# Masks, one-hot and class table in bfloat16, the table in three parts, and the class product in the middle of a split

## The reference, cut to what matters

```python
h = jnp.maximum(_layernorm(x, axis=-1), 0.0)          # x: 32 x 256 x 1024
x = x + _L0_gnn_ref(h, adj, b1, adj, b2)              # adj: 256 x 256, used as W1 and W2

def _construct_adj(x, k):                             # x: 8 x 256 x 1024 in the names
    fv = x.mean(axis=1)
    nf = fv / jnp.linalg.norm(fv, axis=1, keepdims=True)
    sim = nf[:, :, None] * nf[:, None, :]
    _, idx = jax.lax.top_k(sim, kk + 1)
    idx = idx[..., 1:]
    adj = jnp.zeros((Bn, Nn, Nn), x.dtype).at[b_ix, r_ix, idx].set(1.0)
    adj = jnp.maximum(adj, jnp.swapaxes(adj, 1, 2))
    adj = adj.at[:, d, d].set(1.0)
    return adj

def _gc(x, adj, W, b):
    deg = adj.sum(axis=2, keepdims=True)
    deg = jnp.where(deg == 0, jnp.ones_like(deg), deg)
    h = x @ W.T + b
    return jnp.einsum('bij,bjh->bih', adj / deg, h)

adj = _construct_adj(x, K)                            # K = 8
h = jax.nn.relu(_gc(xr, adj, W1, b1))                 # xr: the last two axes swapped
h = _gc(h, adj, W2, b2)
```

## Time and profile before

| | |
|---|---|
| median of 3 runs | 516.86 us (516.5 to 517.17) |
| the profiled execution's own time | 516.86 us |
| its span in the profile | 515.0 us |
| TensorE, matmuls | 485.7 us busy, 94% |
| TensorE, weight loads | 334.0 us, 65% |
| VectorE | 367.8 us, 71% |
| GpSimd | 371.9 us, 72% |
| ScalarE | 339.1 us, 66% |
| chain that ended last | PE 86%, DVE 7%, ACT 2%, DMA 2%, POOL 1% |

### The profile page before, as it was taken

The page is one execution under the profiler, slowest core; times in us unless marked ns, Lnnn a source line. Parts: engine busy times, 40 slices in busy tenths (PEclk is TensorE's granted clock), DMA queues, the critical chain, the costliest instruction groups (busy, mean ns, idle before and its releaser), DMA issues.

```text
span 515.0 us, 7290 instructions
## 1 busy us (share of the span) xinstructions
PE 485.7 (94%) x2416; PEld 334.0 (65%) x2416; DVE 367.8 (71%) x858; ACT 339.1 (66%) x692; POOL 371.9 (72%) x342
## 2 busy tenths in 40 slices
PE   1974999899999999999999999999999999999996
PEld 0253667667776677767777677767777677776774
DVE  4899797989776977779776978769776764522334
ACT  3844988547778577766778676775778655555551
POOL 0182658666888877787888777787887788778773
PEclk9995899899999999999999999999999999999999
DMA  8892274355656365565565465664624243444424
GB/s 315 305 405 91 81 292 183 146 208 227 257 200 232 152 252 202 233 227 197 194 238 214 192 252 205 246 247 162 251 93 164 86 178 150 164 164 164 163 83 163
DMA packets 27701, 102.74 MB, mean 199 GB/s; under 512 B 2064, under 2 KB 2576, under 8 KB 27664
## 3 DMA queue, kind: packets, MB, share of 16 engines
q1 hardware_dynamic: 27280, 101.23, 51.6%
q0 software_dynamic: 384, 1.05, 0.5%
HBM read 68.72 MB, written 33.55 MB: 199 GB/s over the span
## 4 chain that ended last, share of the span: by engine, by line
PE 86%; DVE 7%; ACT 2%; DMA 2%; POOL 1%; issue 1%; SPq 0%; DVEq 0%; POOLq 0%; ACTq 0%
PE ps L589 46%; PE ps L595 23%; PE ps L619 5%; PE aux L556 5%; PE aux L651 3%; DVE stats L715 2%; DMA xin<-x 2%; PE aux L578 1%; DVE code_r L779 1%; PE ps L626 1%; ACT r L355 1%; PE aux L565 1%; DVE onehot L788 1%; ACT hb L321 0%; POOL h_lo L449 0%
## 5 line engine op out<-in xcount | busy, mean ns | idle before, releaser
L460 POOL TENSOR_TENSOR r_lo<-r,r_hi 128x512 fp32r<-128x512 f32 x128 | 167.7, 1332 | 88.6 <-ACT r_hi L378 84.2
L449 POOL TENSOR_TENSOR h_lo<-hb,h_hi 128x512 fp32r<-128x512 f32 x128 | 166.8, 1326 | 7.9 <-ACT h_hi L341 7.8
L892 DVE SCALAR_TENSOR_TENSOR res<-ps,bias,res 128x512 f32<-128x512 f32 x128 | 90.1, 746 | 66.5 <-PE ps L626 66.4
L321 ACT ACTIVATE hb<-xin,nmean,rstd 128x1024 f32<-128x1024 f32 x64 | 79.0, 1235 | 52.7 <-DVE nmean L736 52.7
L589 PE MATMUL ps<-r_hi,w_hi 128*128 128x512 f32 x256 | 109.7, 429 | 1.9 <-ACT r_hi L370 1.9
L589 PE MATMUL ps<-r_hi,w_lo 128*128 128x512 f32 x256 | 102.6, 401 | 0.0
L589 PE MATMUL ps<-h_hi,w_hi 128*128 128x512 f32 x256 | 101.9, 398 | 0.0
L589 PE MATMUL ps<-h_hi,w_lo 128*128 128x512 f32 x256 | 101.2, 395 | 0.0
L361 ACT ACTIVATE r<-ps,beta 128x512 f32<-128x512 f32 x64 | 43.5, 684 | 63.5 <-PE ps L619 63.5
L715 DVE BATCH_NORM_STATS2 stats<-xin 128x6 f32<-128x512 f32 x128 | 78.9, 676 | 5.4 <-DMA xin<-x 5.4
L595 PE MATMUL ps<-h_lo,w_hi 128*128 128x512 f32 x256 | 73.4, 408 | 0.0
(11 more groups left out here) (87 smaller groups left out, 543.8 us busy)
## 6 DMA issues: line engine op xcount, KB each, us to landing
res<-x SPq DMA_DIRECT2D x32, 1024.0 KB, 4.8
xin<-x SPq DMA_DIRECT2D x31, 1024.0 KB, 7.3
out<-res SPq DMA_DIRECT2D x31, 1024.0 KB, 4.0
xin<-x SPq DMA_DIRECT2D x2, 512.0 KB, 3.8
out<-res SPq DMA_DIRECT2D x4, 256.0 KB, 2.1
w<-w_t SPq DMA_DIRECT2D x1, 256.0 KB, 8.2
cst<-small SPq DMA_DIRECT2D x1, 229.5 KB, 5.5
xg<-x_t,rows POOLq DMA_INDIRECT x8, 5.7
```

The costliest lines, as they stand in the source:

```text
L321: last = nc.scalar.activation(hb[:, a, kf], xin[:, b % NX, kf], ACT.Relu, bias=nmean[:, kf, e:e + 1], scale=rstd[:, kf, e:e + 1], accum_ou ...
L449: last = nc.gpsimd.tensor_tensor(h_lo[:, kf, n], hb[:, b % NH, kf, n], h_hi[:, kf, n].bitcast(F32), ALU.subtract)
L460: last = nc.gpsimd.tensor_tensor(r_lo[:, kf, n], r[:, kf, n], r_hi[:, kf, n].bitcast(F32), ALU.subtract)
L892: nc.vector.scalar_tensor_tensor(res[:, b % NR, m, n], bank[m][:], bias2[:, m:m + 1], res[:, b % NR, m, n], ALU.add, ALU.add).then_inc(out ...
```

## The change

- `onehot`, `mask`, `tab` and `v_hi` are bfloat16 instead of fp32r.
- As bfloat16 holds 8 bits of a value, the table comes in three parts on 24 rows of each quadrant instead of two on 16: `cls`, `less` and `rows_of` are widened, a constant `less2` is new, `src3` holds three copies, the class matmuls have 24 weight columns instead of 16. `table` has four instructions instead of two, each waiting for the one before: `v_hi` from V2, the difference to `REST` in PSUM, `v_mid` from `REST`, and `tab`.
- `products(t+1)` on GpSimd stands between the two instructions of `split_h(t+2, 0)`, from pass 2 to the pass before the last but one, rather than after them; `tables` goes to the front of its pass.
- `group_twin` and `group_counts` also write a sum (`beside`), which nothing reads.
- The last element of `code_r` takes one of its operands from `ZERO` in PSUM, written by an additional instruction in `top_first`, instead of from `code` in SBUF.

```diff
--- before.py
+++ after.py
-        ("cls", np.where(row < 16, row % 8, -1.0)[:, None]),
-        ("less", np.where((row >= 8) & (row < 16), -1.0, 0.0)[:, None]),
+        ("cls", np.where(row < 24, row % 8, -1.0)[:, None]),
+        ("less", np.where((row >= 8) & (row < 24), -1.0, 0.0)[:, None]),
+        ("less2", np.where((row >= 16) & (row < 24), -1.0, 0.0)[:, None]),
...
-        onehot = sb("onehot", [P, 2, 2, N], F32R)
+        onehot = sb("onehot", [P, 2, 2, N], BF16)
...
-        mask = sb("mask", [P, P], F32R)
+        mask = sb("mask", [P, P], BF16)
...
+        beside = sb("beside", [P, 2])
...
-        src3 = sb("src3", [P, KF, 2 * NCLS])
-        v_hi = sb("v_hi", [P, P], F32R)
-        tab = sb("tab", [P, P], F32R)
+        src3 = sb("src3", [P, KF, 3 * NCLS])
+        v_hi = sb("v_hi", [P, P], BF16)
+        v_mid = sb("v_mid", [P, P], BF16)
+        tab = sb("tab", [P, P], BF16)
...
+        REST = aux[:, 2 * P:3 * P]
+        ZERO = aux[:, P + K_TOP:P + K_TOP + 1]
...
         def rows_of(b, m):
             a = 32 * ((b % G + 2 * m) % G)
-            return slice(a, a + 2 * NCLS)
+            return slice(a, a + 3 * NCLS)
...
-            def split_h(b, h):
+            def split_h(b, h, between=None):
                 n = half_of(h)
                 pool.wait_ge(hhi_ready, nth(b, h))
                 for kf in range(KF):
+                    if kf == 1 and between is not None:
+                        products(between)
...
             for t in range(-1, LAST):
+                if t > 0 and (t + 1) % G == 0:
+                    tables((t + 1) // G)
                 if t == 1:
                     gather(1)
                 split_r(t + 1, 0)
-                if t == 1:
-                    products(2)
-                if t >= 0 and t + 2 < NB:
-                    split_h(t + 2, 0)
-                if t > 0 and (t + 1) % G == 0:
-                    tables((t + 1) // G)
-                if t != 1:
+                if 1 < t < LAST - 1:
+                    split_h(t + 2, 0, t + 1)
+                else:
+                    if t == 0:
+                        split_h(2, 0)
                     products(t + 1)
+                    if t == 1:
+                        split_h(3, 0)
                 split_r(t + 1, 1)
...
-                nc.vector.tensor_scalar(STAT, fv[:, 1:K_TOP + 1], 0.0, 6.0, ALU.is_equal, ALU.add).then_inc(static_ready, 1)
+                nc.vector.tensor_scalar(STAT, fv[:, 1:K_TOP + 1], 0.0, 6.0, ALU.is_equal, ALU.add)
+                nc.vector.tensor_scalar(ZERO, fv[:, 0:1], 0.0, 4.0, ALU.is_equal, ALU.add).then_inc(static_ready, 1)
...
-                nc.vector.scalar_tensor_tensor(code_r[:, N - 1:N], fv[:, 0:1], 0.0, code[:, 0:1], ALU.min,
+                nc.vector.scalar_tensor_tensor(code_r[:, N - 1:N], fv[:, 0:1], 0.0, ZERO, ALU.min,
...
-                nc.vector.tensor_scalar(cnt_d[:], c_("pick_n"), cnt[:], None, ALU.mult).then_inc(cntd_ready, 1)
+                nc.vector.tensor_scalar(cnt_d[:], c_("pick_n"), cnt[:], None, ALU.mult, ALU.add,
+                                        accum_out=beside[:, 0:1]).then_inc(cntd_ready, 1)
...
-                last = nc.vector.tensor_scalar(onehot[o, k % 2, 1], code_r[q], c_("cls")[q], None, ALU.is_equal)
+                last = nc.vector.tensor_scalar(onehot[o, k % 2, 1], code_r[q], c_("cls")[q], None, ALU.is_equal, ALU.add,
+                                               accum_out=beside[o, 1:2])
...
-                    src3[:].rearrange("p k (d c) -> p k d c", d=2),
-                    prod[:].unsqueeze(2).broadcast_to([P, KF, 2, NCLS, NSRC]), AX_X, ALU.add).then_inc(src3_ready, 1)
+                    src3[:].rearrange("p k (d c) -> p k d c", d=3),
+                    prod[:].unsqueeze(2).broadcast_to([P, KF, 3, NCLS, NSRC]), AX_X, ALU.add).then_inc(src3_ready, 1)
...
                 nc.vector.tensor_copy(v_hi[:], V2).then_inc(vhi_ready, 1)
-                dve.wait_ge(vhi_ready, b + 1)
-                nc.vector.scalar_tensor_tensor(tab[:], v_hi[:].bitcast(F32), c_("less"), V2,
-                                               ALU.mult, ALU.add).then_inc(tab_ready, 1)
+                dve.wait_ge(vhi_ready, 3 * b + 1)
+                nc.vector.scalar_tensor_tensor(REST, v_hi[:], c_("less"), V2, ALU.mult, ALU.add).then_inc(vhi_ready, 1)
+                dve.wait_ge(vhi_ready, 3 * b + 2)
+                nc.vector.tensor_copy(v_mid[:], REST).then_inc(vhi_ready, 1)
+                dve.wait_ge(vhi_ready, 3 * b + 3)
+                nc.vector.scalar_tensor_tensor(tab[:], v_mid[:], c_("less2"), REST, ALU.mult, ALU.add).then_inc(tab_ready, 1)
```

More of the change, by code:

```diff
@@ L444, in _, with products @@
         def _(pool):
-            def split_h(b, h):
+            def products(b):
+                e, gp, g = b % RB, (b // G) % 2, b % G
+                shape = [P, KF, NCLS, NSRC]
+                pool.wait_ge(mix_ready, b // G + 1)
+                pool.wait_ge(r_ready, 2 * nth(b, 1))
+                if b > 0:
+                    pool.wait_ge(src3_ready, b)
+                nc.gpsimd.tensor_tensor(
+                    prod[:], src2[:, :, e].unsqueeze(2).broadcast_to(shape),
+                    mix[:, gp, g].unsqueeze(1).broadcast_to(shape), ALU.mult).then_inc(prod_ready, 1)
+            def split_h(b, h, between=None):
                 n = half_of(h)
```

## The result

The changed kernel took 521.79 us (median of 4 runs, 520.39 to 523.36) against 517.01 for the kernel before beside it (516.5 to 517.22): a ratio of 1.0097 (its 95% interval [1.0071, 1.0124]), 4.8 us slower. The profiled execution of it is the one of 520.39, 1.4 under the median, with a span of 518.6; before it was 515.0 in 516.86.

What follows compares the result with a forecast made beforehand. TensorE was taken to bound the kernel from about 105 us on. Terms 11.7 - 1.7 + 0.2 + 0.8 - 2.3 = +8.7 us, on a span of 515.0 plus 1.9 around it, gave 525.6 us; range 519 to 531.

Steps and rivals of the forecast that it cites:

- Table chain: Two added dependent VectorE instructions ahead of tab, 0.65 us for both against 0.31 of slack: +11.7 us over all batches.
- Ordinary steps: Table chain in 13 batches such as 2, 3, 7, 11: 0.34 us of new waiting each, 12 counted, 4.1 us.
- batches 4, 8, ...: Table chain where VectorE comes late out of the search: 0.87 us in each of five batches, 4.35 us.
- batches 5, 9, ...: Table chain where the earlier product frees v_hi: terms at 2.03 instead of 2.08, five times -0.05, -0.25 us.
- Quads: The 62 groups of four added-term matmuls, now bfloat16: 0.03 us less each, less 0.2 where VectorE sets the time, -1.7 us.
- Rival 1: In the quads, bfloat16 weights load about twice as fast, gaining 0.08 us a quad rather than 0.03: 522.5 us; chance 0.20.
- Rival 3: In the 62 quads, bfloat16 loses most of the 0.39 that is not stream, 0.25 each: 512.0 us, faster; chance 0.10.
- V2: Class matmuls load 24 columns instead of 16, hidden but for the first of each step: +0.2 us (0 to 0.6).
- Start: First two twins take longer with a sum beside them, so masks and all behind come later: +0.8 us (0.3 to 3).
- Group 1: Shorter code_r element and cnt_d nearly close TensorE's 2.15 us wait and avoid the half clock: net -2.3 us (0 to -4).
- Rival 2: Group 1's gain fails: another wait takes the place of cnt_d and the clock falls anyway: 527.9 us; chance 0.15.
- Moves on GpSimd: tables ahead of a split that waits anyway, products in mid-split with cover for the work queued behind: 0 us.

Runs made afterwards that it cites:

- e1: The kernel before with one-hot, mask, v_hi and tab in bfloat16 only, still two parts on 16 rows (third part missing from the result): 509.79 us, ratio 0.988.
- e3: The kernel before with only ZERO in PSUM and the sums beside cnt_d and the twins: 514.88 us, ratio 0.9977.
- e4: The changed kernel with GpSimd's loop of the kernel before (tables and products where they stood): 523.93 us, ratio 1.0145.
- e5: The changed kernel without the sums beside cnt_d and the twins, ZERO kept: 522.18 us, ratio 1.0109.
- e6: The changed kernel with code in SBUF back in place of ZERO, the sums kept: 521.84 us, ratio 1.0096.
- e2: The kernel before with the four-instruction table chain in fp32r on 16 rows, table still made from v_hi: 528.24 us, ratio 1.0225.
- e8: The kernel before with class matmuls in mid high product, and VectorE's reduction ahead of the search, its end a pass later: 515.47 us, ratio 0.9984.
- e7: The changed kernel with class matmuls in mid high product, and VectorE's reduction ahead of the search, its end a pass later: 509.61 us, ratio 0.9863.
- e9: The changed kernel with only VectorE's reordering: reduction ahead of the search, end of the search after table: 518.88 us, ratio 1.0034.
- e10: The changed kernel with only TensorE's reordering: class matmuls in the middle of the high product: 514.95 us, ratio 0.9963.

## Why the prediction was right, and where it was off

I forecast 525.6 us (519 to 531), slower with 0.85. It is slower, within the range, and 3.8 us less than forecast. The direction came by the mechanism forecast, a longer chain in front of the terms. That the number is no further off is in part luck: the quads gained 5.0 us more than forecast, and the chain cost 1.8 more. By steps:

- **Table chain: +11.7 forecast, +13.5 measured** (the shifts of the terms over batches 0 to 30, summed, without batch 2). The mechanism held in every kind of step. The two instructions added 0.72, not 0.65: the subtraction takes 0.36 and the cast 0.29, and each gap is 0.04. Ordinary steps lost 0.43 (I said 0.34), batches 0 and 1 0.73 (0.65), batches 4, 8, ... 0.82 (0.87), batch 24 0.56 (0.56), batches 5, 9, ... 0.03 (-0.05), batches 6, 10, ... 0.40 (0.33), batch 31 nothing. Groups of instructions by form in the changed kernel, columns as in the earlier trace rows:

```profile
L887 DVE TENSOR_REDUCE src<-prod 128x48 f32<-128x432 f32 x32 | 19.2, 599 | 9.5 <-POOL prod L458 9.5
...
L895 DVE SCALAR_TENSOR_TENSOR aux<-v_hi,cst,aux 128x128 f32<-128x128 bf16 x32 | 11.4, 356 | 1.1
...
L636 PEld LDWEIGHTS ps<-onehot,tab 24*128 24x128 bf16 x128 | 6.0, 90 | 16.2 <-DVE tab L899 15.5 <-issue 0.7
```

The third copy in the reduction cost the 0.15 that I gave it (599 against 450 ns). The waits of TensorE on VectorE in the changed kernel (us, times, longest):

```profile
PE ps L636 <- DVE tab L899: 5.2, 8, 1.5
...
PE aux L661 <- DVE src L887: 0.6, 1, 0.6
```

I had said that it would show some 25 waits of 0.35. This view alone would have misled: it shows 5.2 us in 8 waits, since the pipelined masks still count as busy while the terms wait. The weight loads' idle time before the terms, 15.5 us, is nearer to it, and the distances between starts tell it.
- **Quads: -1.7 forecast, -6.7 measured.** This is the step that failed. The sum took 0.03 a quad "near the lower end, because the drains and the fp32r load behind the quad stay". They do stay: the matmul behind the quad, whose 0.50 against 0.40 I had priced, still takes 0.50 in e1. What went is the same wait in the quad's own matmuls, 0.49 in the earlier trace rows: they take 498 ns on average before and 385 in e1, and terms to next product is 0.32, not the 0.39 to 0.42 that I said the profile would show. The quad's own load falls from 183 to 90 ns, which covers most of that; no run separates the rest, about 0.02, from faster streaming. Rival 1 named the mechanism and still halved the wrong thing: some 0.10 of the load of 0.18 stood bare, so a load shorter by 0.09 takes away nearly the whole wait on the way into the quad and none on the way out, where the load is still fp32r. Its 522.5 is near the 521.79 measured, but other terms had a share in that. The rule of the Trainium skill cited there ("TensorE: Matmul & The Clock Gate", Weight-path perf modes) speaks of about 2x, and the trace agrees, 183 to 90 ns. Rival 3 (0.25 a quad, the other side) did not come: 0.108 is short of its 0.17.
- **V2: +0.2**, measured 31 x 0.007 = 0.2; it is contained in the shifts of the terms above.
- **Start: +0.8 forecast, none in the profile.** The first masks came 12.41 after the codes instead of 11.53, as said, but the class matmuls of batch 0 stood at 55.76 against 56.15: a stretch of half clock of the same length, 17.1 us, had begun and ended 1.4 earlier. Counted from the codes they came at 20.16, before at 20.29. In e3 and e4, which have the same sums, the stretch ended at 55.82 and 56.64, as late as before (55.88) or later, and the 0.8 was paid: 21.04 and 21.13.
- **Group 1: -2.3 forecast, -2.3 measured** (batch 2 to batch 3, 18.55 to 16.25), with what I named next in line: VectorE's reduction now comes last (102.33) and the class matmuls wait 0.6 for it. The exact agreement is luck. By e5 and e6 ZERO and the sum on `cnt_d` are 1.8 of it; the absence of the half clock is some 0.7 (I said 1.4), by e1; the late table of batch 2 takes 0.4 back, and two quads give 0.2. That the edits kept the clock up isn't shown. TensorE had idled 2.15 us for `cnt_d` in the kernel before, 1.73 in e2 and 2.18 in e8, and the clock fell behind it; in e1 it idled 2.26 and the clock did not fall. Rival 2 fell, as the clock stayed at full in 96.20 to 100.00 and the wait that came in the place was 0.6 us.
- **Moves on GpSimd: 0 forecast outside batches 5, 6, ..., which held.** I credited it with curing the lateness of batches 5 and 6 and their like. e2 and e4 show that the longer steps cure most of that by themselves: in e4 all of it in batches 6, 10, ... and half in 5, 9, ... (`v_hi` at 1.01 instead of 1.38). Its gain at batch 28 (0.7 us) I hadn't seen.

By stretches the two profiles differ by -0.39 us up to the class matmuls of batch 0, +1.13 from there to those of batch 2, -2.30 to batch 3, +5.34 to batch 31 and -0.22 to the end: +3.56, where I forecast +8.7. The longest stretch closes by its terms: 12.05 for the chain in batches 3 to 30, less 6.05 for 56 quads, less 0.64 for the wait at batch 28, is 5.36. So the change trades 6.4 us of cheaper weight loads for some 12 of a longer chain, and stays slower because the chain ended just ahead of its consumer: 0.31 of slack for 0.72 of new work.

## What to carry to other kernels

Price an added dependent instruction at its consumer: its duration less the slack there, in each kind of step, and then look again at which other waits the longer step has healed, since two latenesses in one loop don't add up. Where a type change needs more preparation, move the producer earlier in the same edit (e7): that turned 4.8 us of loss into 7.2 of gain. For an operand type that the trace doesn't have, subtract what the load would lose from the part of it that stands bare, rather than scale the wait, and look at the matmuls that use this load, not at the ones behind them.

## What was unexpected of the hardware

- A weight load of 128 columns in bfloat16 takes 90 ns, in fp32r 183 to 190. Between the terms and the next product that is worth 0.108 us, though the product behind loads fp32r as before.
- While GpSimd works, a VectorE instruction on a single element with both tensors in SBUF took 1.17 to 1.18 us; with one of them in PSUM it took 0.14. With GpSimd idle (126.29 us in the kernel before) both in SBUF took 0.15. `cnt_d`, 32 elements, took 0.92 to 1.11 plain in group 1 and 0.24 to 0.25 with a sum written beside it.
- That sum has a price elsewhere: 1024 elements took 1.27 us with it, and at the start two plain ones took 0.98 together in bfloat16 (1.51 in fp32r); a plain one takes 1.45 where GpSimd works.
- The start holds a stretch of half clock in every profile (37.4 to 54.5 us in the changed kernel), and five profiles (e2, e6, e7, e9, e10) have a second one of 3.4 us near 60. A third place is near 97 us, where the clock fell behind an idle of 2.15 us in the kernel before and not behind one of 2.26 in e1. A difference of 1 us between two such kernels is read from distances within the profile, not from totals.
